# Layer-1 edge pass: ScalarE scales the carried state by the eight heads' factors, in place of VectorE

## What is computed

```
e = (edge_attr @ We).reshape(-1, H, C)
k_j = k[src] + e
v_j = v[src] + e
alpha = jnp.sum(q[dst] * k_j, axis=-1) / jnp.sqrt(C)
amax = jax.ops.segment_max(alpha, dst)
ex = jnp.exp(alpha - amax[dst])
denom = jax.ops.segment_sum(ex, dst)
out = jax.ops.segment_sum(v_j * (ex / denom[dst])[:, :, None], dst)
```

## Time and profile before

| | us |
|---|---|
| median of 3 runs | 5898.32 (5891.51 to 5899.26) |
| the profiled execution | 5889.27 |
| its span in the profile | 5887.5 |
| VectorE busy | 3811.9 (65%) |
| GpSimd busy | 3381.2 (57%) |
| TensorE busy | 2894.1 (49%) |
| ScalarE busy | 1441.5 (24%) |

### The profile page before, as it was taken

How to read it: one execution, slowest core, us unless ns; L and a number is a source line. 1 busy time by engine, 2 the same in 40 slices (tenths; PEclk the granted TensorE clock), 3 DMA queues, 4 the chain that set the end, 5 groups by cost and what they waited for, 6 DMA issues and landing times. The chain is left out here.

```text
span 5887.5 us, 49851 instructions
## 1 busy us (share of the span) xinstructions
PE 2894.1 (49%) x13052; PEld 2231.5 (38%) x13052; DVE 3811.9 (65%) x6117; ACT 1441.5 (24%) x2526; POOL 3381.2 (57%) x3382
## 2 busy tenths in 40 slices
PE   7513200000000000036888858588888888885777
PEld 5412200000000000035555523477777777774456
DVE  7357778885555545456332345599999999995763
ACT  1123323331333333211222211122222222221320
POOL 0267767777777777572320246677777777773200
PEclk9655555555555555565999979799999999996888
DMA  3033353332353333233321224799999999994113
GB/s 97 35 94 106 106 175 106 107 108 78 108 214 107 107 112 111 85 100 113 102 86 55 85 95 176 243 324 324 324 324 323 324 324 324 324 324 134 64 50 138
DMA packets 289926, 961.77 MB, mean 163 GB/s; under 512 B 79009, under 2 KB 119592, under 8 KB 248229
## 3 DMA queue, kind: packets, MB, share of 16 engines
q0 software_dynamic: 171296, 483.60, 27.2%
q1 hardware_dynamic: 118484, 476.59, 24.3%
HBM read 626.03 MB, written 345.69 MB: 165 GB/s over the span
## 5 line engine op out<-in xcount | busy, mean ns | idle before, releaser
L1235 PE MATMUL e_psE<-e_we,e_eaT 128*128 128x256 f32 x3136 | 900.0, 413 | 266.1 <-DVE e_wv L1134 142.3
L1097 POOL DMA_INDIRECT e_kv<-kv,rec x784 | 875.4, 1117 | 267.4 <-issue 238.5
L765 POOL DMA_INDIRECT g_g<-t,rec x784 | 775.0, 989 | 278.4 <-issue 278.1
L765 POOL DMA_INDIRECT g_g<-t,dst_of x784 | 743.3, 948 | 259.3 <-issue 257.5
L1235 PEld LDWEIGHTS e_psE<-e_we,e_eaT 128*128 128x128 f32 x3136 | 646.8, 209 | 387.0 <-ACT e_eaT L1178 286.3
L1393 PE MATMUL j_psM<-ident,tail 128*128 128x128 f32 x32 | 7.5, 429 | 1150.0 <-PEq L53 1150.0
L1236 PE MATMUL e_psE<-e_kv,ident 128*128 128x256 f32 x1568 | 507.9, 408 | 0.0
L802 DVE TENSOR_TENSOR_SCAN g_wv<-g_fx,g_wv 128x2176 f32<-128x2176 f32 x98 | 459.0, 4683 | 0.4 <-issue 0.4
L1393 PEld LDWEIGHTS j_psM<-ident,tail 128*128 128x128 f32 x32 | 7.0, 330 | 1150.8 <-issue 1150.8
L1104 POOL DMA_INDIRECT e_q<-q,q_of x392 | 370.6, 945 | 119.4 <-issue 119.4
L942 ACT ACTIVATE g_st<-g_wv 128x2048 f32<-128x2048 f32 x98 | 375.9, 3836 | 0.0
(11 more groups left out here) (513 smaller groups left out, 6546.1 us busy)
## 6 DMA issues: line engine op xcount, KB each, us to landing
state<-e_st SPq DMA_DIRECT2D x98, 1088.0 KB
e_ea<-in_edge_attr SPq DMA_DIRECT2D x98, 896.0 KB, 9.4
state_f<-g_st SPq DMA_DIRECT2D x49, 1088.0 KB, 4.3
state_b<-g_st SPq DMA_DIRECT2D x49, 1088.0 KB, 4.2
m_work<-xs SPq DMA_DIRECT2D x119, 128.0 KB, 2.2
ys<-m_work SPq DMA_DIRECT2D x119, 128.0 KB, 1.7
xs<-g_ta SPq DMA_DIRECT2D x28, 512.0 KB
g_g<-t,rec POOLq DMA_INDIRECT x784
```

Of the source, the lines that this page charges most:

```text
L765: pool.indirect_dma_start(g[:, u, j, :], None, tab, bass.IndirectOffsetOnAxis(ap=at_, axis=0)).then_inc(gat[u], 16)
L1097: pool.indirect_dma_start(kv[:, u, b, :], None, c.kv, bass.IndirectOffsetOnAxis(ap=c.rec[:, t, 1:2], axis=0)).then_inc(gkv[u][b // 4], 16)
L1235: nc.tensor.matmul(half, eaT[:, m, j, k, :], we[:, k, :], start=(k == 0), stop=False)
```

## The change

The instruction of line 1154 on VectorE is taken out, together with the drain behind it. In its place ScalarE runs eight `activation` copies behind the exponential, one for each head: each takes 32 columns of the last state of the block before, and scales them by the head's carry factor, which it reads from column 0 of `cw`. A new semaphore, `carried`, tells VectorE that they are done; VectorE waits for it ahead of the product of factor and denominator. ScalarE waits for its own exponential before it reads the factors.

```diff
-        marked, act_mt = sem("marked"), sem("act_mt")
+        marked, act_mt, carried = sem("marked"), sem("act_mt"), sem("carried")
...
-                    of_head = lambda b: cw[:, :, b].unsqueeze(2).to_broadcast([P, H, C])
...
                     tt(weighed, weighed, cw[:, :, 1:B1].rearrange("p h b -> p b h").unsqueeze(3).to_broadcast([P, B, H, C]),
                        ALU.mult)
-                    tt(by_head(before[:]), by_head(st[:, 1 - u, B - 1, 0:D]), of_head(0), ALU.mult)
-                    v.drain()
+                    v.wait_ge(carried, blk + 1)
                     tt(cw[:, :, 0], cw[:, :, 0], den[:, :, B], ALU.mult)
...
                 nc.scalar.activation(cw[:].rearrange("p h b -> p (h b)"), ex[:].rearrange("p h b -> p (h b)"),
                                      ACT.Exp).then_inc(cwd, 1)
+                act.wait_ge(cwd, blk + 1)
+                for h in range(H):
+                    last = nc.scalar.activation(before[:, h * C:(h + 1) * C], st[:, 1 - u, B - 1, h * C:(h + 1) * C], ACT.Copy,
+                                                scale=cw[:, h, 0:1])
+                last.then_inc(carried, 1)
                 act.wait_ge(dnd, blk + 1)
```

## The result

The changed kernel is slower: a median of 5948.73 us (5945.21 to 5956.67, 6 runs) against 5895.15 us (5891.51 to 5899.26, 6 runs) of the kernel before, ratio 1.0092, 95% interval [1.0079, 1.0105]. That is 54 us more, where 35 us less were forecast.

The account below looks back on a forecast made before the run. VectorE was taken to bound the layer-1 edge pass at 16.40 us a block, with DMA next. A DMA-limited 31 us plus 4 us from gather reserve gave 35 us off: 5854 profiled, 5863 median, range 5843 to 5890.

Parts of the forecast that it names:

- VectorE sets the 16.40 us: Layer-1 edge pass: VectorE's nearly gapless chain sets the 16.40 us block, so what leaves its chain leaves the block.
- a met wait: VectorE's new wait before old line 1156: already met, it costs nothing, so 0.50 us a block is saved.
- the full saving: Line 1154 and its drain off VectorE in the edge pass: 0.50 us a block, 98 blocks, 49 us.
- ScalarE's copies: Eight copies behind ScalarE's exponential, 0.24 us each, 1.92 us in all, done 0.29 us before wanted, hidden by line 1152.
- rival (d): ScalarE's copies in the edge pass end late, at 429 ns each: slower than before by 71 us; chance 0.07.
- 15.0 is under 15.9, so GpSimd is not next: Edge pass: GpSimd's 12 gather issues of 1.25 us take 15.0 us a block, under VectorE's shortened 15.90.
- DMA lets a block fall to 16.08 us: Edge pass: with share 1.03 as full, DMA has 0.32 us spare a block, limiting that part of the gain to 31 us.
- Rival (b): Edge pass: DMA gives way and all of the saving stays, 49 us, 5849 us; chance 0.34.
- The range and the chances: Whole kernel: 5843 to 5890 us; chances 0.77 faster, 0.16 within 12 us, 0.07 slower.

Follow-up runs that it names:

- the fourth experiment: The kernel before the change, with VectorE's weights' product (line 1152) cut into four pieces of 512 columns: 5919.55 us against 5890.88, ratio 1.0044.

## Why the prediction was wrong, step by step

- *VectorE sets the 16.40 us:* right. Line 1154 and its drain were worth 0.51 us (0.50 forecast), a met wait cost nothing, and with GpSimd out of the way (one gather fewer, or two pieces) the block fell to 15.91 and 15.99 us, and the time by 43 and 40 us, of the 49 that the full saving was put at.
- *ScalarE's copies:* hidden, as forecast. They end 0.4 us before they are wanted:

```profile
4407.26 0.26 ACT L1191 ACTIVATE e_cw<-e_ex 128x72 f32<-128x72 f32 x1 [3.40 <-DVE e_ex L1148]
4407.56 1.80 ACT L1195 ACTIVATE e_before<-e_st,e_cw 128x32 f32<-128x32 f32 x8
```

```profile
L1195 ACT ACTIVATE e_before<-e_st,e_cw x784: 304/306/322, 3766.5 to 5417.2; 128x32 f32<-128x32 f32 x196
```

  I took 0.24 us each without overlap, 1.92 in all; it was 0.306 us each, overlapping, 1.80 in all. The price of the Trainium skill, "ScalarE: Activation LUTs" (it stands in the section "What ACT_TABLE_LOAD costs"), was exact on both. Its rule to multiply on VectorE ("Rules for kernel authors") did not decide here: rival (d) has the right sign by luck, since ScalarE was never late.
- *"15.0 is under 15.9, so GpSimd is not next":* this is the step that failed. I read the row of 2.13 us for 0.95, saw that it met line 1152, and set it down as a stretch beside a round of 15.0 us. It was a hold whose length depends on when the issue comes. A round of 15.0 + 1.4 us, equal to the block already, was the warning, for in 800 us of the kernel before GpSimd waited for nobody:

```profile
POOL e_kv L1097 <- issue: 118.8, 390, 0.3
...
POOL e_q L1104 <- issue: 59.7, 196, 0.3
...
PEld e_psT L1225 <- DMA e_ea<-ea_tail: 1.1, 2, 0.8
```

  Its 16.4 us agreed with VectorE's because the hold took up the difference; with the hold cut short, the same kernel's GpSimd waits 1.2 us a block (the fourth experiment). Over 93 rounds of GpSimd before and 94 after, from the first key gather of a block to that of the next, the means before are 15.0 us of issues, 1.10 of hold in the product, 0.25 of smaller holds and 0.04 of waits, 16.40 in all with rounding. After, they are 15.0, 1.70, 0.13 and 0.18, 17.01 in all. At 15.9 us there is room for a hold of 0.7 us, and 0.91 is the least that a whole product gives, so 15.9 was out of reach. That least hold would still give a round near 16.1 us and a gain; the loss comes from the mean of 1.70, which is measured and not derived.

  The Trainium skill, "SBUF — State Buffer", section "SBUF: two separate sides", states that a VectorE operation with two SBUF inputs and a GpSimd operation that reads SBUF exclude each other for a whole instruction, whichever starts first. The traces agree for the product: an issue 0.08 us behind its start is held for 2.1 us, and the sum with one input holds none. They do not agree for the issue: the one at 4418.50 runs on for 0.67 us beside the product that starts at 4418.77, and that product takes its usual 2.29 us. That the issue of a gather counts as an operation that reads SBUF is an inference from the hold. The prediction does not use the rule.
- *DMA lets a block fall to 16.08 us:* mis-sized, 0.32 us of spare where the runs show 0.49 or more, and the reason is the share. It stood at 1.00 to 1.02 at 308, 323, 331 and 332 GB/s, so it did not tell how much room there was. Nor did 1.05 at the highest rate mark a full engine: another of the 34 windows of the earlier trace rows reads 1.18 at 262 GB/s.

```profile
4435.00:4436.00 1.00, 1.00 (x6) 0.89 (x5) 0.93 (x1) 0.04 (x1) 0.91 (x1) 1.00 1.18 262
```

  The DMA engines kept up at 15.91 us a block and took nothing back; where their limit lies, no run shows. That no engine that computes waits for DMA was nearly right: TensorE did, 1.1 us in 800 (the row of line 1225 above). Rival (b) judged the DMA engines rightly. The Trainium skill, "Perfetto Trace Analysis", section "Identifying the Most-Contended Engine", calls the occupancy of sixteen DMA engines misleading, and under "What 'DMA-bound' means" it names the engine that issues as a bound of its own. The trace agrees: after the change GpSimd's issues and the 0.30 us or so ahead of each fill 786 of the 800 us from 4000 on.
- *The range and the chances:* the slower side had 0.07, all of it for ScalarE being late. The rival that came true, a third engine's round made longer by the shorter block, was not among them.

What stays open: why the mean hold settles at 1.70 us rather than elsewhere between 0.91 and 2.16. It moves from block to block, and no run fixed the phase.

## What to carry to other kernels

Before a chain is shortened, look for an engine whose round has the same length without waiting on a semaphore: its time may be stretched by a hold that adapts, and its free round plus the least possible hold is the least that the next bound can be; here the mean hold was 0.8 us above the least, which turned a gain into a loss. Where one engine's long instruction holds another's short ones, cut it: here two pieces cost 0.08 us a block and took the mean hold from 1.70 to 0.29 us. In the kernel before, where VectorE set the pace, the same kind of cut only cost. A DMA share of 1.00 is no bound by itself; look for who waits for a landing, and for who waits for nobody.

## What the runs showed of the hardware that was not expected

- In the changed kernel's trace 96 gather issues of GpSimd start 0.05 us or more inside the VectorE product with two SBUF inputs. All of them end 0.81 to 0.84 us after that product, and the longest takes 3.06 us for 0.95. One that starts 0.11 us or more ahead takes at most 1.01 us, and does not lengthen the product. Three issues start 0.04 us inside: they pass in 0.95 us, and those products take 2.37 us for 2.29. The state steps (line 1162), with two SBUF inputs as well, 0.48 us each and a drain between them, hold an issue for at most 0.20 us in the kernel before; no run shows why so little. Between two back-to-back pieces the issue gets through (1.32 us with four pieces, 1.25 with two):

```profile
4418.95 1.25 POOL L1097 DMA_INDIRECT e_kv<-kv,rec  x1 [0.30 <-issue]
```

- The share of the DMA engines read 1.00 to 1.02 from 308 to 332 GB/s, and 0.88 at 281 GB/s, when about a tenth of the bytes was taken away.
